# Block products for a second pair of chunks from tile 4 on, with new orders of work, in a fused FFN and long-convolution kernel

## The chip, the cores and the metric

The kernel runs on one core of a Trainium2 chip. The time is the device time of one execution in microseconds. The engines are PE (TensorE, matmuls), DVE (VectorE), ACT (ScalarE), POOL (GpSimd) and SP (SyncE, which here only issues DMAs). Each engine takes its instructions in the order of the program and waits on semaphores.

## The reference

x has 4 x 512 = 2048 tokens of 512 features. The result is x plus a long convolution plus a gated FFN, both of the layer-normed x:

```python
xn = _layernorm(x, axis=-1)
x = x + s4_convolution(xn) + ffn(xn)
# ffn, with NF4 weights of M = 1792, an absmax for each 64 codes:
g = jnp.einsum('bsh,mh->bsm', xn, Wg)
u = jnp.einsum('bsh,mh->bsm', xn, Wu)
h = jax.nn.silu(g) * u
out = jnp.einsum('bsm,hm->bsh', h, Wd)
# the convolution: its kernel K (512 long) is made from 64 complex poles,
# a Cauchy sum and an inverse FFT; y = irfft(rfft(u) * rfft(K)) + D * u
```

## The kernel before, in words

All products are made of three fp16 matmuls (high x high, high x low, low x high), so each weight and each activation is split into a high and a low half. M is cut into 14 tiles of 128 (k = 0 to 13), the tokens into four chunks of 512 (c = 0 to 3). For a tile and a chunk a gate product and an up product are wanted, of 12 matmuls of 128x512 each.

**Direct and block products.** For tiles 0 to 2 (the opening) all is direct. From tile 3 on, chunks 2 and 3 (side s = 0) are made together by seven block products of 6 matmuls in place of 8 (gate and up of two chunks taken as 2 x 2 blocks). Chunks 0 and 1 (side s = 1) have them from FIRST_BLOCKED[1] on, tile 5 in the kernel before. Block products need sums of the weights (up_sums, other_sums on DVE, then block_hi on ACT and block_lo on DVE) and, once, sums of the tokens of the pair: token_whole, token_sum and token_lo on DVE, token_hi on ACT, four of each for a side. Per tile and side ACT copies two products between banks (copy_m1, copy_m5) and DVE adds two (join). silu is on ACT, h_mul on DVE. The high half of h of chunk 0 is made by ACT (h_hi) where the chunk is direct, by POOL where it is blocked; h_lo is DVE's.

**Windows.** PE works through a mixed_window(k) while side 1 is direct, and a blocked_window(k) after that. In blocked_window(k) the order is products 1, then product 4 of the tile before, then 5, 6, 2, 3, 7, each for both sides; the first blocked window has no product 4. DVE, ACT and POOL each have an order written out by hand for the same windows.

**Units.** Each weight tile is a unit that is dequantised while earlier tiles multiply: SEQ lists the units, two for each of the tiles 3 to 12 (up of tile k+1, gate of tile k+2), then those of the down weights (GU and above). EARLY_IN names the windows in which one unit of the down weights is made in addition, so that made_in(k) is 3 there and 2 elsewhere; made_before(k) is the first unit of window k. For a unit SP loads codes (codes_of) and scales (absmax_of), POOL makes first_pass, ACT five or six passes (chain), DVE step WHOLE and step SCALED, POOL weight_hi (from unit 7 on, ACT before) and DVE weight_lo of the unit before. On POOL first_pass(u + 2) stands before weight_hi(u). On DVE the three operations of a unit are its items; eighths() spreads the items of a window over eight slots, and ACT's passes likewise.

**The load queue.** SP goes through the units in order:

```python
for place in range(8, UNITS - 3):
    codes_of(place + 1)
    if place > 8:
        absmax_of(place)
    if place == LINE_AT:
        toeplitz()
```

toeplitz() waits for the convolution's line (DVE, end of window 11), writes it to DRAM as 128 shifted copies (L629), waits until that has landed, and reads it back as the matrix T (L634). DVE takes T's maximum in the last slot of window 12 (L1894), then makes other_sums(13), block_lo(13, 0) and the joins of tile 12.

**The opening.** x is loaded in eight pieces of two token tiles (load_x). stats, moments and twelve small rstd steps for four token tiles give the normalisation; norm(t) applies it (ACT for t = 0, POOL for the others), turn(t) transposes a token tile on PE for t below 8, x_hi and x_lo split it. v_step and exp_step on POOL are small steps of 128x1 to 128x8 for the convolution's kernel.

## Time and profile before

| | us |
|---|---|
| median of 3 runs | 459.49 |
| lowest, highest | 458.85, 459.49 |
| profiled execution | 460.08 |
| its span | 458.3 |
| PE busy | 438.2 |
| DVE busy | 398.4 |
| ACT busy | 278.8 |
| POOL busy | 214.6 |

All times of rows are microseconds from the start of the span. A row of the timeline has the start, the duration, the engine (SPq is the load queue), the line of the kernel, the operation with its output and inputs, the count if several are merged, and in brackets the idle time before it with what ended that time. A helper has one line for all its calls, so an operation is told from its neighbours by its place in the order. A PE row's duration includes the drain of its last matmul.

### The profile page before, as it was taken

What the parts mean: (1) busy time and instruction counts of PE and PEld (TensorE: products, weight loads), DVE (VectorE), ACT (ScalarE), POOL (GpSimd) and SP (SyncE); (2) the same over time, 40 slices, a digit from 0 to 9 for tenths busy, and PEclk for the clock granted to TensorE, in tenths of its full rate; (3) what the DMA queues carried; (4) which work ended last, traced back from release to release, by engine and by line L of the source; (5) the groups of instructions that cost most, each with busy time, mean ns of one, the idle gap of its engine ahead of it and who ended that gap; (6) DMA issues with size and microseconds to landing.
All of it is one profiled execution on the core that took longest, in us unless ns stands there. A gap on an engine that the chain in (4) does not pass through costs nothing.

```text
span 458.3 us, 7272 instructions
## 1 busy us (share of the span) xinstructions
PE 438.2 (96%) x2560; PEld 248.8 (54%) x2560; DVE 398.4 (87%) x641; ACT 278.8 (61%) x472; POOL 214.6 (47%) x163
## 2 busy tenths in 40 slices
PE   1879999999999999999999999999999999999997
PEld 1534444443444444434444444466544788888886
DVE  5988979969889798999897879879996999999993
ACT  7868594295877759588684787856032542445340
POOL 2777299547456848669646847778100000000000
PEclk9989999999999999999999999999999999999999
DMA  8543636022315415155222233457691021101111
GB/s 291 172 131 139 144 75 182 1 92 71 138 47 183 161 47 200 54 183 191 63 69 65 61 80 101 111 187 249 193 369 60 1 94 47 46 1 48 47 47 46
DMA packets 34168, 51.41 MB, mean 112 GB/s; under 512 B 13076, under 2 KB 14164, under 8 KB 33364
## 3 DMA queue, kind: packets, MB, share of 16 engines
q1 hardware_dynamic: 34132, 50.95, 35.3%
q8 instruction: 20, 0.33, 0.3%
q14 instruction: 16, 0.13, 0.1%
HBM read 38.03 MB, written 10.81 MB: 107 GB/s over the span
## 4 chain that ended last, share of the span: by engine, by line
PE 85%; DVE 6%; ACT 2%; issue 2%; DMA 2%; POOL 1%; SPq 0%; DVEq 0%; ACTq 0%; POOLq 0%
PE bank L2264 33%; PE bank L2391 21%; PE bank L2109 16%; PE bank L2341 8%; PE bank L2331 6%; ACT work L936 1%; DMA h<-in_x 1%; DVE h L1438 1%; DVE work L1313 1%; DMA work<-in_q_gate 1%; DVE w L1323 1%; DVE work L1309 1%; PE bank L2145 0%; DVE h L1412 0%; POOL h L845 0%
## 5 line engine op out<-in xcount | busy, mean ns | idle before, releaser
L936 ACT ACTIVATE work<-work 128x512 f32<-128x512 f32 (+1 forms) x234 | 130.0, 628 | 11.5 <-POOL work L845 7.8
L845 POOL TENSOR_SCALAR work<-work 128x512 f32<-128x512 int32 x39 | 85.9, 2202 | 64.4 <-DVE work L1309 46.1
L2264 PE MATMUL bank<-h 128*128 128x512 f16 x360 | 81.5, 379 | 0.9 <-ACT bank L1029 0.9
L2109 PE MATMUL bank<-xT,w 128*128 128x512 f16 (+1 forms) x300 | 66.2, 377 | 2.3 <-DVE w L1323 1.1
L2264 PEld LDWEIGHTS bank<-h 128*128 128x128 f16 x360 | 34.9, 98 | 44.0 <-ACT bank L1029 2.4
L2391 PE MATMUL bank<-wd,work 128*128 128x256 f16 x504 | 56.2, 273 | 0.0
L2264 PE MATMUL bank<-xT,w 128*128 128x512 f16 x240 | 55.4, 379 | 0.0
L2391 PEld LDWEIGHTS bank<-wd,work 128*128 128x128 f16 (+1 forms) x504 | 49.3, 98 | 6.0
L2109 PEld LDWEIGHTS bank<-xT,w 128*128 128x128 f16 x300 | 29.4, 99 | 36.8 <-DVE w L1323 2.4
L1250 ACT ACTIVATE work<-h 128x896 f16<-128x896 f32 x30 | 27.9, 942 | 28.4 <-DVE h L2017 18.3
L2391 PE MATMUL bank<-h,work 128*128 128x256 f16 x378 | 42.2, 273 | 0.0
L858 POOL TENSOR_SCALAR w<-work,sc 128x512 f16<-128x512 f32 x21 | 39.0, 1857 | 6.6 <-DVE work L1313 5.6
L2391 PEld LDWEIGHTS bank<-h,work 128*128 128x128 f16 x378 | 37.0, 98 | 4.3
L2264 PEld LDWEIGHTS bank<-xT,w 128*128 128x128 f16 x240 | 23.4, 98 | 28.1
L2341 PE MATMUL bank<-wd,h 128*128 128x512 f16 x168 | 36.4, 379 | 0.0
L1309 DVE SCALAR_TENSOR_TENSOR work<-work 128x512 f32<-128x512 f32 x39 | 28.4, 729 | 5.1 <-ACT work L936 5.1
L2003 DVE TENSOR_TENSOR work<-h,work 128x896 bf16<-128x896 f32 x30 | 32.5, 1083 | 0.1
L1313 DVE SCALAR_TENSOR_TENSOR work<-work 128x512 f32<-128x512 f32 x41 | 29.9, 730 | 1.5
L1029 ACT ACTIVATE bank<-bank 128x512 f32<-128x512 f32 x20 | 11.6, 582 | 31.7 <-DVE work L1438 15.6
L1020 ACT ACTIVATE work<-bank,sc 128x512 f32<-128x512 f32 x36 | 24.6, 684 | 9.9 <-PE bank L2109 9.9
L2264 PE MATMUL bank<-xT,h 128*128 128x512 f16 x120 | 28.1, 379 | 1.2 <-DVE bank L1412 1.0
L858 POOL TENSOR_SCALAR wd<-work,sc 128x512 f16<-128x512 f32 x14 | 26.3, 1877 | 4.7 <-DVE work L1313 3.8
...
## 6 DMA issues: line engine op xcount, KB each, us to landing
...
```

The lines of the kernel that those rows point to most:

```text
L845: pool.tensor_scalar(chain_room(u, "r"), qs[:, u % 2, :], RIGHT_FROM, RIGHT_FROM, ALU.max, ALU.subtract).then_inc(first_done, 1)
L858: pool.tensor_scalar(weight_of(u)[HI], whole_of(u), scale_of(u), None, ALU.mult).then_inc(phi_done, 1)
L936: nc.scalar.activation(room, qs[:, u % 2, :] if j == 0 else room, KNEE, scale=scale, bias=bias, alpha=below).then_inc(knee_done, 1)
L1250: nc.scalar.activation(slot_of(o)[:, HI], src, ACT.Copy).then_inc(o_hi, 1)
L1309: ins = v.scalar_tensor_tensor(whole, left, CHAIN_TOP if u in CHAINED else LEFT_TOP, right, ALU.min, ALU.add)
L1313: ins = v.scalar_tensor_tensor(whole, whole, CHAIN_STEP if u in CHAINED else -LEFT_TOP, am[:, u % 2, :], ALU.add, ALU.mult)
L2003: v.tensor_tensor(slot[:, LO].bitcast(BF16), src, slot[:, HI], ALU.subtract).then_inc(o_lo, 1)
L2109: mm = nc.tensor.matmul(out_b, weights(k)[:, unit, wl, f, :], xT[:, TPC * c + first:TPC * c + last, xl, f, :], start=(i == 0), stop=(i == ...
L2264: mm = nc.tensor.matmul(out_b, weight(wl, f), token(xl, f), start=(n == 0 and i in (1, 5)), stop=(n == 5), skip_group_check=i not in (1, 5))
L2331: mm = nc.tensor.matmul(bank[(t + 4) % 8][:, P * j:HD], xT[:, t, xl, j, :], tz[:, tl, 0:HD - P * j], start=(n == 0), stop=(n == 3 * NC - 1))
L2341: mm = nc.tensor.matmul(bank[(t + 4) % 8][:], part, wd[:, mt, wl, :], start=(mt == 0 and n == 0), stop=(mt == NM - 1 and n == 2))
L2391: mm = nc.tensor.matmul(out_b, part, w, start=(n == 0), stop=(n == 3 * KT - 1))
```

## The change

FIRST_BLOCKED[1] becomes 4: side 1 has block products from tile 4 on. There is one mixed window now, that of tile 3. EARLY_IN becomes (7, 9, 11, 12): the window of tile 8 makes two units and that of tile 12 three. With it made_before(12), and so LINE_AT, become one less (30 and 31). The first token sum of side 1 stands in the opening, the other three and token_lo(1, 0) in tile 3. In tile 3 weight_lo(9) stands before the steps of unit 10 (LO_SOONER). In the windows of two blocked sides h_mul of chunk 0 stands behind one slot of items instead of two. In the opening ACT makes norms 0, 1 and 4 (ACT_NORMS), POOL the others; x 2 and 3 are loaded later; the gate product of tile 1 stands before turn(4) on PE; stats, scales, weight halves and passes stand in another order; warm_up has 12 matmuls instead of 16; and the first fourteen v_steps on POOL stand behind first_pass(8).

```diff
@@ -39,7 +39,7 @@
 BLOCKED = range(3, NM)
 BLOCKS = (1, 5, 2, 6, 3, 7, 4)
 ROLE_B, ROLE_E = (2, 0), (3, 1)
-FIRST_BLOCKED = (3, 5)
+FIRST_BLOCKED = (3, 4)
 A_BANK, E_BANK, B_BANK = (4, 0), (5, 1), (6, 2)
@@ -119,7 +119,7 @@
-EARLY_IN = (7, 8, 9, 11)
+EARLY_IN = (7, 9, 11, 12)
 EARLY = len(EARLY_IN)
 SEQ = list(range(9))
 for k in range(3, NM - 1):
@@ -560,7 +560,12 @@
         RSTD = 12
         SUMMED = (1,)
-        POOL_NORMS = 1
+        ACT_NORMS = (0, 1, 4)
+        LO_SOONER = made_before(3) + 1
+
+        def pool_norms(t):
+
+            return t + 1 - sum(1 for i in ACT_NORMS if i <= t)
         ACC = 4
         WEIGHT_SCALES = 9
@@ -662,11 +667,11 @@
             load_x(1)
             load_codes(1, q_up[0])
             sp.dma_start(amf, am_flat).then_inc(amf_ld, 16)
-            load_x(2)
-            load_x(3)
             load_absmax(0, am_gate[0])
             load_codes(2, q_gate[1])
+            load_x(2)
             load_absmax(1, am_up[0])
+            load_x(3)
             load_codes(3, q_up[1])
             load_absmax(2, am_gate[1])
             sp.dma_start(cols[:], s4_cols).then_inc(s4_ld, 16)
@@ -867,16 +872,15 @@
                 pool.tensor_scalar(sums_room(SEQ[u] // 2)[0], whole_of(u), scale_of(u), None, ALU.mult).then_inc(g_done, 1)
             first_pass(1)
-            for t in range(POOL_NORMS, TPC):
-                norm(t)
+            norm(2)
+            norm(3)
             first_pass(2)
             first_pass(3)
             first_pass(4)
-            for t in range(TPC, 2 * TPC):
-                norm(t)
+            norm(5)
+            norm(6)
+            norm(7)
             first_pass(5)
-            for i in range(14):
-                v_step(i)
             first_pass(6)
             for t in range(2 * TPC, 3 * TPC):
                 norm(t)
@@ -884,6 +888,8 @@
             for t in range(3 * TPC, NT):
                 norm(t)
             first_pass(8)
+            for i in range(14):
+                v_step(i)
             for i in range(EXP_STEPS):
                 exp_step(i)
             for u in POOL_HALVES:
@@ -1037,7 +1043,7 @@
                 act.wait_ge(xs_done[s], (1, 3, 2, 4)[i])
                 if i == 0:
                     if s == 0:
-                        act.wait_ge(xp_done, NT - POOL_NORMS)
+                        act.wait_ge(xp_done, pool_norms(NT - 1))
                     else:
                         act.wait_ge(xlo_done, NT)
                 nc.scalar.activation(tk[s][:, i, HI].rearrange("p f t -> p (f t)"), x_sums[s][(1, 2, 0, 3)[i]],
@@ -1067,7 +1073,7 @@
                                      ACT.Copy).then_inc(hhi_done, 1)
             def norm(t):
-                act.wait_ge(rs_step, RSTD)
+                act.wait_ge(rs_step, RSTD * (t // TPC + 1))
                 nc.scalar.activation(xnb[:, t % 8, :], xs[:, t, :], ACT.Identity, scale=rs[:, 4, t:t + 1],
                                      bias=rs[:, 5, t:t + 1]).then_inc(xn_done, 1)
@@ -1090,7 +1096,7 @@
                     act.wait_ge(tp_done, t + 1)
                     src, dst = bank[4 + t % TPC][:], xT[:, t, HI].rearrange("p c f -> p (c f)")
                 else:
-                    act.wait_ge(xp_done, t - POOL_NORMS + 1)
+                    act.wait_ge(xp_done, pool_norms(t))
                     src, dst = xnb[:, t % 8, :], xst[:, t % 8, HI, :]
                 nc.scalar.activation(dst, src, ACT.Copy).then_inc(xhi_done, 1)
@@ -1099,11 +1105,12 @@
             stats(1)
             chain(1, 0, 5)
             norm(0)
+            norm(1)
             chain(1, 5, 6)
+            chain(2, 0, 1)
+            weight_hi(0)
             x_hi(0)
-            weight_hi(0)
             x_hi(1)
-            chain(2, 0, 1)
             x_hi(2)
             x_hi(3)
             chain(2, 1, 2)
@@ -1111,25 +1118,26 @@
             chain(2, 2, 6)
             chain(3, 0, 2)
             weight_hi(2)
-            chain(3, 2, 4)
+            chain(3, 2, 6)
+            norm(4)
+            silu(0)
+            act.wait_ge(b_mm, 1)
+            nc.scalar.activation(yv[:, 0:2], bank[3][:, 0:2], ACT.Copy).then_inc(b_cp, 1)
+            weight_hi(3)
             x_hi(4)
-            chain(3, 4, 6)
-            silu(0)
-            chain(4, 0, 1)
-            weight_hi(3)
+            chain(4, 0, 2)
             x_hi(5)
             x_hi(6)
-            act.wait_ge(b_mm, 1)
-            nc.scalar.activation(yv[:, 0:2], bank[3][:, 0:2], ACT.Copy).then_inc(b_cp, 1)
             x_hi(7)
-            chain(4, 1, 6)
+            chain(4, 2, 6)
+            silu(1)
             h_hi(0)
-            silu(1)
+            chain(5, 0, 3)
             weight_hi(4)
-            chain(5, 0, 6)
+            chain(5, 3, 6)
             h_hi(1)
+            x_hi(8)
             silu(2)
-            x_hi(8)
             weight_hi(5)
             x_hi(9)
             x_hi(10)
@@ -1169,26 +1177,18 @@
             def mixed_window(k):
                 n = NCH * k
-                if k > 3:
-                    silu(n)
-                    copy_m1(0, k)
-                    part(k, 0, 2)
                 h_hi(n)
                 copy_m5(0, k)
-                if k == 3:
-                    items(ACT_AT[9] - 3, ACT_AT[9])
-                    part(k, 0, 2)
-                else:
-                    token_hi(1, 0)
-                part(k, 2, 3)
+                items(ACT_AT[9] - 3, ACT_AT[9])
+                part(k, 0, 3)
                 silu(n + 2)
                 part(k, 3, 5)
                 silu(n + 1)
+                token_hi(1, 0)
                 part(k, 5, 6)
                 silu(n + 3)
                 part(k, 6, 8)
-                if k > 3:
-                    part(k + 1, 0, 2)
+                part(k + 1, 0, 2)
                 block_hi(k + 1, 0)
                 block_hi(k + 1, 1)
@@ -1327,7 +1327,7 @@
                 for p in range(first, last):
                     u, i = item_of(DVE_AT, p)
                     if u in CHAINED:
-                        i = (3, 4, 2)[i]
+                        i = ((2, 3, 4) if u == LO_SOONER else (3, 4, 2))[i]
                     if i != 2:
                         step(u, i if i < 2 else i - 1)
                     elif u > 0:
@@ -1377,7 +1377,7 @@
                 if s == 0 and f == 0:
                     dve.wait_ge(xt_ld[c - 2], 16 * TPC)
                 elif s == 1 and i == 2:
-                    dve.wait_ge(xp_done, NT - POOL_NORMS)
+                    dve.wait_ge(xp_done, pool_norms(NT - 1))
                 elif s == 1 and i == 0:
                     dve.wait_ge(xt_ld[1], 16 * TPC)
                 hi, lo = (xT[:, TPC * c:TPC * c + TPC, l, f:f + 2, :] for l in (HI, LO))
@@ -1566,64 +1566,64 @@
             rstd(0, 3)
             rstd(0, 4)
             rstd(0, 5)
-            step(0, WHOLE)
+            scales(1)
             rstd(0, 6)
             rstd(0, 7)
             rstd(0, 8)
-            scales(1)
+            scales(2)
             rstd(0, 9)
-            scales(2)
+            scales(3)
             rstd(0, 10)
-            scales(3)
+            scales(4)
             rstd(0, 11)
-            scales(4)
             dve.wait_ge(id_done, 1)
             scales(5)
-            stats(4)
             scales(6)
+            step(0, WHOLE)
             step(0, SCALED)
-            step(1, WHOLE)
             scales(7)
             scales(8)
+            step(1, WHOLE)
+            weight_lo(0)
             x_lo(0)
-            weight_lo(0)
             x_lo(1)
             step(1, SCALED)
             x_lo(2)
             x_lo(3)
             weight_lo(1)
+            stats(4)
             stats(5)
             stats(6)
+            step(2, WHOLE)
+            step(2, SCALED)
             stats(7)
             moments(4, 8)
+            weight_lo(2)
             rstd(1, 0)
             rstd(1, 1)
             rstd(1, 2)
             scales(9)
             rstd(1, 3)
+            scales(10)
             rstd(1, 4)
+            scales(11)
             rstd(1, 5)
-            step(2, WHOLE)
+            scales(12)
             rstd(1, 6)
             rstd(1, 7)
             rstd(1, 8)
-            step(2, SCALED)
+            step(3, WHOLE)
             rstd(1, 9)
             rstd(1, 10)
             rstd(1, 11)
-            weight_lo(2)
+            step(3, SCALED)
+            h_mul(0)
+            weight_lo(3)
             stats(8)
             x_lo(4)
-            scales(10)
-            step(3, WHOLE)
-            scales(11)
-            step(3, SCALED)
-            h_mul(0)
-            scales(12)
-            weight_lo(3)
+            stats(9)
             x_lo(5)
             x_lo(6)
-            stats(9)
             x_lo(7)
             stats(10)
             stats(11)
@@ -1648,13 +1648,13 @@
             step(5, WHOLE)
             step(5, SCALED)
             h_lo(1)
+            x_lo(8)
             stats(12)
-            x_lo(8)
-            stats(13)
             weight_lo(5)
             x_lo(9)
             x_lo(10)
             x_lo(11)
+            stats(13)
             h_mul(2)
             stats(14)
             stats(15)
@@ -1703,6 +1703,7 @@
             token_lo(0, 2)
             token_whole(1, 1)
             h_mul(10)
+            token_sum(1, 0)
             token_lo(0, 1)
             weight_lo(7)
             up_sums(BLOCKED[0], 7)
@@ -1718,34 +1719,24 @@
                     items(eighths(DVE_AT, k, first), eighths(DVE_AT, k, last))
                 n = NCH * k
-                if k == 3:
-                    h_mul(n)
-                    h_lo(n)
-                    join(0, k, 0)
-                    part(0, 5)
-                    join(0, k, 1)
-                    h_mul(n + 3)
-                    part(5, 6)
-                else:
-                    part(0, 2)
-                    token_sum(1, 1)
-                    h_mul(n)
-                    part(2, 3)
-                    h_lo(n)
-                    part(3, 4)
-                    join(0, k, 0)
-                    token_sum(1, 2)
-                    token_lo(1, 0)
-                    part(4, 6)
-                    join(0, k, 1)
-                    h_mul(n + 3)
-                token_sum(1, 0 if k == 3 else 3)
+                h_mul(n)
+                h_lo(n)
+                join(0, k, 0)
+                part(0, 2)
+                token_sum(1, 1)
+                part(2, 5)
+                join(0, k, 1)
+                h_mul(n + 3)
+                token_sum(1, 2)
+                token_lo(1, 0)
+                part(5, 6)
                 part(6, 7)
                 other_sums(k + 1)
                 h_mul(n + 1)
                 block_lo(k + 1, 0)
                 h_mul(n + 2)
                 block_lo(k + 1, 1)
+                token_sum(1, 3)
                 part(7, 8)
             def window(k, stage=None):
@@ -1763,9 +1754,9 @@
                     h_mul(n + 1)
                     block_lo(k, 1)
                     h_mul(n + 2)
-                    stage_of(0, 2)
+                    stage_of(0, 1)
                     h_mul(n)
-                    stage_of(2, 4)
+                    stage_of(1, 4)
                     join(0, k, 0)
                     stage_of(4, 5)
                     h_lo(n)
@@ -2135,25 +2126,25 @@
             nc.tensor.transpose(bank[0][0:3, 0:P], amx, ident[:]).then_inc(mx_tp, 1)
             def turn(t):
-                if t < POOL_NORMS:
-                    pe.wait_ge(xn_done, t + 1)
-                else:
-                    pe.wait_ge(xp_done, t - POOL_NORMS + 1)
+                if t in ACT_NORMS:
+                    pe.wait_ge(xn_done, ACT_NORMS.index(t) + 1)
+                else:
+                    pe.wait_ge(xp_done, pool_norms(t))
                 if t >= TPC:
                     pe.wait_ge(xlo_done, t - TPC + 1)
                 for f in range(NC):
                     mm = nc.tensor.transpose(bank[4 + t % TPC][:, P * f:P * f + P], xnb[:, t, P * f:P * f + P], ident[:])
                 mm.then_inc(tp_done, 1)
-            warm_up(10)
-            turn(0)
+            warm_up(8)
             pe.wait_ge(one_done, 1)
             pe.wait_ge(sc_done, 7)
             nc.tensor.matmul(bank[0][:, P:P + 6], ones[:], dg3, start=True, stop=True).then_inc(mx_bc, 1)
+            turn(0)
             turn(1)
             turn(2)
             turn(3)
-            warm_up(6)
+            warm_up(4)
             pe.wait_ge(wlo_done, 1)
             pe.wait_ge(xlo_done, 2)
@@ -2165,8 +2156,8 @@
             for i in range(2):
                 mm = nc.tensor.matmul(bank[3][:, i:i + 1], vcs[:, P * i:P * i + P], bps, start=True, stop=True)
             mm.then_inc(b_mm, 1)
+            products(1, (0,))
             turn(4)
-            products(1, (0,))
             turn(5)
             turn(6)
             turn(7)
```

## Rows read from the trace of the kernel before

**Rows 1.** The page: busy time, share of the span and instructions of each engine.

```profile
PE 438.2 (96%) x2560; PEld 248.8 (54%) x2560; DVE 398.4 (87%) x641; ACT 278.8 (61%) x472; POOL 214.6 (47%) x163
```

**Rows 2.** PE's waits, whole span: line, releaser: us, times, longest.

```profile
PE bank L2145 <- POOL h L749: 2.9, 1, 2.9
PE bank L2109 <- DVE w L1323: 1.1, 1, 1.1
PE bank L2264 <- DVE bank L1412: 1.0, 1, 1.0
PE bank L2264 <- ACT bank L1029: 0.9, 1, 0.9
```

**Rows 3.** Busy time by stretch: PE, PEld, DVE, ACT, POOL, clock, DMA, GB/s.

```profile
83.00:90.00 7.00, 7.00 (x34) 3.14 (x32) 7.00 (x9) 0.84 (x2) 3.61 (x2) 1.00 0.00 0
...
143.04:161.17 18.13, 18.13 (x85) 8.23 (x84) 15.21 (x26) 13.03 (x25) 14.16 (x9) 1.00 0.45 151
...
179.66:200.11 20.45, 18.47 (x85) 8.05 (x84) 18.99 (x30) 15.82 (x31) 15.63 (x9) 1.00 0.38 124
```

**Rows 4.** One microsecond of the opening: PE busy, granted clock, DMA.

```profile
28.00:29.00 1.00, 1.00 (x3) 0.50 0.00 0
```

**Rows 5.** Timeline of the opening: start, us, engine, line, operation, count, idle.

```profile
25.74 1.09 DVE L1323 SCALAR_TENSOR_TENSOR w<-work,sc,w 128x512 f16<-128x512 f32 x1 [0.32 <-ACT w L963]
26.88 4.45 PE L2109 MATMUL bank<-xT,w 128*128 128x512 f16 x12
...
33.01 12.26 PE L2109 MATMUL bank<-xT,w 128*128 128x512 f16 x56 [0.37 <-ACT yv L1123]
...
34.24 0.68 DVE L1551 TENSOR_TENSOR xT<-bank,xT 128x512 f16<-128x512 f32 x1
```

**Rows 6.** Timeline: small steps and weight halves on POOL, weight_lo(7) on DVE.

```profile
34.62 0.29 POOL L805 TENSOR_SCALAR V<-yv,cols 128x2 f32<-128x2 f32 x1
...
72.20 2.39 POOL L771 TENSOR_SCALAR sc<-sc 128x1 f32<-128x1 f32 x1
...
76.30 0.19 POOL L775 TENSOR_TENSOR sc<-sc 128x1 f32<-128x1 f32 x1
...
79.48 2.24 POOL L858 TENSOR_SCALAR w<-work,sc 128x512 f16<-128x512 f32 x1
...
88.61 0.74 DVE L1323 SCALAR_TENSOR_TENSOR w<-work,sc,w 128x512 f16<-128x512 f32 x1
```

**Rows 7.** Timeline: a token sum, block_lo(3,0), and PE's products 5 and 6 of tile 3.

```profile
80.86 1.21 DVE L1395 TENSOR_TENSOR h<-h 128x1024 f32<-128x1024 f32 x1
...
92.66 0.58 DVE L1369 SCALAR_TENSOR_TENSOR h<-h,sc 128x256 f16<-128x256 f32 x1
...
93.89 2.75 PE L2264 MATMUL bank<-h 128*128 128x512 f16 x12
```

**Rows 8.** Timeline: h_mul of chunk 0 in tile 8's window.

```profile
188.36 0.74 DVE L1438 SCALAR_TENSOR_TENSOR work<-bank,sc,h 128x512 f32<-128x512 f32 x1
```

**Rows 9.** Timeline of the load queue: issues around the line's transfer (L629).

```profile
254.70 1.10 SPq L609 DMA_DIRECT2D work<-in_am_down  x2
257.25 0.32 SPq L629 DMA_DIRECT2D lines<-wd  x1
...
271.13 0.37 SPq L603 DMA_DIRECT2D work<-in_q_down  x1
```

**Rows 10.** Timeline of tile 12's end and tile 13's beginning.

```profile
273.31 0.69 DVE L1894 TENSOR_REDUCE sc<-wd 128x1 f32<-128x512 f32 x1 [2.20 <-DMA wd<-lines]
...
274.23 1.95 POOL L845 TENSOR_SCALAR work<-work 128x512 f32<-128x512 int32 x1 [5.34 <-DMA work<-in_q_down]
...
275.46 0.68 DVE L1412 TENSOR_TENSOR h<-bank,h 128x512 f32<-128x512 f32 x1
...
276.27 2.08 POOL L858 TENSOR_SCALAR wd<-work,sc 128x512 f16<-128x512 f32 x1
...
278.25 2.75 PE L2264 MATMUL bank<-h,w 128*128 128x512 f16 x12
```

## The prediction

> **What bounds the kernel now.** I read the busy times first: TensorE (PE) is busy 96% of the span [rows 1]. Then PE's waits, longest first [rows 2]: 2.9 us in the opening for a normalised tile from POOL, 1.1 us for a low weight half from DVE (tile 4), and 1.0 and 0.9 us for DVE's join and ACT's copy (both in tile 8). Past 33 us PE waits for about 3.5 us in all, so the kernel is a chain of matmuls with four small holes. The stretches by stage say who is nearly late [rows 3]: DVE is busy 7.00 of 7 us before tile 3 and 18.99 of 20.45 in tile 8, while tile 6 (18.13 us for 14 products of 6 matmuls, so 0.216 us a matmul) has 3 us of DVE to spare. So every edit is read twice: what it does to PE, and whether DVE, POOL or the load queue (SP) can still serve PE. The profiled execution took 460.08 us (span 458.3), 0.59 above the median of 459.49; I sum differences from it and put them on the median.
>
> **Fewer matmuls.** Chunks 0 and 1 of tile 4 took 48 matmuls directly and take 7 x 6 = 42 as block products: 6 x 0.216 = -1.3 us on PE, which is the bound. ACT gets four copies where it had two and loses one h_hi to POOL; DVE gets two joins. These lie in the spare time of tile 5's kind of window, which had no PE wait.
>
> **The opening.** Before, PE stood 2.9 us for turn(4), then ran the twelve gate matmuls at a mean of 0.37 us instead of 0.216 [rows 5], with the granted clock at 0.50, which is 1.2 of 2.4 GHz [rows 4]: 1.8 us more. Now the gate product stands ahead of turn(4). I followed the three queues with this trace's durations (0.6 to 0.7 us for an operation of 128x512 on ACT or DVE, 0.86 for a norm on POOL, 0.1 to 0.2 for the four-column steps). On DVE weight_lo(1) ends near 19.1; stats 4 to 6 take 1.9, step 2's two operations 1.4, stats(7) and moments 1.0, and weight_lo(2) ends near 24.0 (before at 26.8 [rows 5]). PE's gate product runs from 24.1 to 26.7. rstd, now behind weight_lo(2), ends near 26.6; turn(4) waits a microsecond for ACT's norm; three norms on POOL end at 29.5 and turn(7) at 30.0. ACT makes x_hi(4), two passes and x_hi 5 to 7 by 32.4, and x_lo(7), which ended at 34.92 [rows 5], ends near 33.4. Chunk 1 can then start at 33.5 instead of 35.6 (33.01 [rows 5] and twelve matmuls): -2.1 us. DVE itself leads by only about 1.6. What I don't see is whether the clock falls again; if it does, the wait for x_lo(7) hides half of it. Bounds: 0.8 to 2.6 us. The cutting of norms to ACT, the later loads of x 2 and 3 (they are read only near 19 us) and the new place of stats cost nothing beyond this.
>
> **The DVE debt before tiles 3 and 4.** token_sum(1,0), 1.2 us like its like [rows 7], now stands before token_lo(0,1), in a stretch where DVE has no idle time [rows 3]. Product 5 of tile 3 started at 93.89, and block_lo(3,0), its last input, ended at 93.24 [rows 7]: 0.65 us of slack. PE comes 2.1 earlier, DVE 1.6 earlier and 1.2 later: a wait of 1.1. In tile 3 DVE gets three more operations of 1.2 us, of which its idle time before the second join hides one or two; block_lo(4,0) then comes 1.0 us late for product 5 of tile 4, and token_lo(1,1) 0.9 late for product 6. The wait of 1.1 us for weight_lo(9) goes, since unit 9 is wanted a window later. Sum to the end of tile 4: -2.1 - 1.3 - 1.1 + 1.1 + 1.0 + 0.9 = -1.5 us.
>
> **Fourteen small POOL steps.** v_step 0 to 13 leave the time at 33 us, where one took 0.29 us, for the place between first_pass(8) and the seventeen exp steps. There a step of the same size took 2.39 us, beside two of DVE's 1.2 us operations [rows 6]. Giving each POOL step the DVE operation that it meets, the exp steps end at 86 to 87 instead of 76.5 [rows 6], first_pass(9) and weight_hi(7) follow, and weight_hi(7), which ended at 81.7 [rows 6], ends near 91.2 on the old axis. DVE wants it for weight_lo(7), which stood at 88.61 [rows 6], now at 89.8. So the old slack of 6.9 us is gone, and 1.4 us more; a little of it is idle time of DVE later in tile 3: DVE, and PE with it, +1.2. Bounds: 0 (each step at 0.29 us, 4.1 us, hidden) to +2.5. The Trainium skill ("GPSIMD Engine Reference", Specifications) says that POOL's way into SBUF is shared with VectorE and is contended by VectorE instructions with two SBUF inputs. The trace agrees (2.39 against 0.29); a reader who held the steps to be free would leave the 1.2 us out.
>
> **Tiles 7 to 9.** Tile 8's window makes two units instead of three, and h_mul of chunk 0, which stood at 188.36 [rows 8] behind two items, now follows h_mul(n+2) at once, some 3 us sooner. ACT's copy comes sooner with it: the 0.9 us goes. Of the 1.0 us for the join, DVE gets 1.4 us back, but PE asks 0.9 sooner: 0.3 to 0.6 may stay. Together -1.6 (bounds -1.3 and -2.0). Tile 9 keeps three units.
>
> **Tile 12, which the change's words don't name.** EARLY_IN now has 12, so window 12 makes units 30, 31 and 32 (before: 31 and 32), and LINE_AT, made_before(12) + 1, falls from 32 to 31. SP thus stops for toeplitz() one unit earlier. Before, the scales of unit 32 went out at 254.70, then the line at 257.25; SP waited for it and only then sent codes, at 271.13, 13.9 us later [rows 9]. Now the codes of unit 33 and the scales of unit 32 are those that wait, while window 12 still needs both: step(32, SCALED) the scales, and weight_hi(31), which stands behind first_pass(33) on POOL, the codes. On the old axis: codes land at 274.2, first_pass runs 274.23 to 276.2, weight_hi 276.27 to 278.35, as unit 34's and 32's did [rows 10]; weight_lo(31) ends at 279.1. Only then comes the maximum of T, which stood at 273.31: DVE is 5.8 us late. The first join behind it stood at 275.46 and took 0.68; it ends at 281.9. Product 4 of tile 12, which waits for that join, stood at 278.25: PE waits 3.7 us. Behind it DVE is ahead again for what product 6 wants. Bounds: 3.0 and 4.5 (ACT's silu and block_hi stand behind the passes of unit 33). Nothing covers this: PE has no other work ahead in its queue.
>
> **The clock there.** PE would stand still in two pieces, with kernel_max between. After 2.9 us of standing in the opening the clock went to 0.50 and cost 1.8 us; here it is 0 to 1.8. I take 0.8. The Trainium skill ("TensorE: Matmul & The Clock Gate", Part 1) has the gate fall to half after an idle stretch, by which the full 1.8 would be due: the sum would be 3.6 and not 2.6.
>
> **Sum.** -1.5 + 1.2 - 1.6 + 3.7 + 0.8 = +2.6 us: 462.7 for a profiled execution like this one, 462.1 for the median.
>
> **Rivals.**
> (a) *Late loads decide, as above*: 461 to 463.5, chance 0.46.
> (b) *Late loads, but POOL's steps are hidden and the clock stays up*: -1.5 - 1.6 + 3.7 = +0.6, 460.1; chance 0.22, half of it within 0.2%. For it: at the pace of 33 us all fourteen take 4.1 us, inside the slack of 6.9. Against: the 2.39.
> (c) *Faster*: the wait at tile 12 doesn't reach PE, because the line's transfer is done sooner or ends before DVE asks. -1.5 - 1.6 with 0 to 1.2 for POOL: 456.4 to 457.6; chance 0.20. For it: DVE idled 2.2 us before T anyway. Against: the order of the queues leaves no way around the 13.9 us.
> (d) *Slower still*: POOL late by 2.5, the full 1.8 of the clock: -1.5 + 2.5 - 1.3 + 3.7 + 1.8 = +5.2, 464.7; chance 0.12. It decides where weight_hi(7) ends later than 92.
>
> The range must leave out no more than 2 in 10: from 457.0 (inside c) to 464.5 (inside d). A difference of 0.2%, 0.9 us, is about what a measurement of this kernel can tell from none. Faster: c and a little of b, 0.21. Same: 0.12. Slower: 0.67.
>
> **What would show it.** A wait of PE of 3 us or more near tile 12's product 4, with SP's codes behind the line's transfer; exp steps that end past 84; no wait of PE in tile 8 over 0.6; chunk 1 starting near 33.5; waits near 1 us at product 5 of tiles 3 and 4. If PE runs through window 13 without a hole, the prediction is wrong at its largest term and the time is near 457. If the opening gives more than 3 us, DVE was not the bound that I make it.

## The result, and the profile after

The changed kernel took 472.63 us (median; 471.01 to 474.97) against 459.17 for the kernel before beside it: a ratio of 1.030, 95% interval 1.025 to 1.034. The forecast was 462.1 with a range of 457.0 to 464.5. The direction was right; the size was missed by 10.5 us, and the time lies outside the range. The profiled execution has a span of 470.6 us, 12.3 more than before.

The page after, busy times, answers [rows 1]. TensorE (PE) has 10 matmuls less in the records (six by the block products, four by the shorter warm_up) and yet 3 us more busy time, in the main by the half clock: 24 matmuls of tile 4 and twelve of tile 12 took 1.7 and 1.5 us more than at full clock. Its share fell from 96 to 94%.

```profile
PE 441.2 (94%) x2550; PEld 249.3 (53%) x2550; DVE 400.4 (85%) x643; ACT 282.6 (60%) x475; POOL 222.5 (47%) x162
```

PE's waits after answer [rows 2] (line, releaser: us in total, times, longest). The 2.9 us for POOL's norm in the opening are gone; 14.2 us of others stand in these rows: for the block's low half (L1369), for joins (L1412, five small ones and a long one), for weight halves (L1323, one of them 1.17 us in the opening) and for the maximum of T (L1885).

```profile
PE bank L2255 <- DVE h L1369: 5.2, 2, 3.8
PE bank L2255 <- DVE bank L1412: 3.3, 5, 1.4
PE bank L2100 <- DVE w L1323: 2.6, 2, 1.4
PE bank L2255 <- DVE h L1412: 2.2, 1, 2.2
...
PE bank L2199 <- DVE sc L1885: 0.9, 1, 0.9
```

Two stretches after, as in [rows 3] (PE, PEld, DVE, ACT, POOL, granted clock, DMA share, GB/s). PE is full in both and runs 6 or 7 matmuls where 9 fit: the clock is at 1.2 of 2.4 GHz.

```profile
116.00:118.00 2.00, 2.00 (x7) 0.65 (x5) 2.00 (x3) 1.94 (x4) 0.00 (x0) 0.50 0.03 8
290.00:292.00 2.00, 2.00 (x6) 0.61 (x5) 1.90 (x4) 1.48 (x3) 0.00 (x0) 0.50 0.41 131
```

**Where the time came from.** I set PE's milestones of the two traces side by side. Chunk 1 starts 1.1 us sooner (34.47 for 35.6). Product 5 of tile 3 is 2.0 late (95.92 against 93.89 [rows 7]); the start of tile 6, 5.5 (148.59 against 143.04 [rows 3]); that of tile 9, 5.2; that of tile 12, 7.0 (264.32 for 257.28); the ones of tile 13, 7.25; and behind product 4 of tile 12 it is 12.1. So there are three places: tiles 3 and 4, tiles 10 and 11, and the line's transfer.

Tiles 3 and 4, timeline after (start, us, engine, line, operation, shape, count, idle before and its releaser):

```profile
73.89 11.46 POOL L776 TENSOR_SCALAR sc<-sc 128x1 f32<-128x1 f32 x9
...
88.89 1.58 POOL L863 TENSOR_SCALAR w<-work,sc 128x512 f16<-128x512 f32 x1
90.51 1.20 DVE L1323 SCALAR_TENSOR_TENSOR w<-work,sc,w 128x512 f16<-128x512 f32 x1 [4.07 <-POOL w L863]
...
91.76 2.76 PE L2100 MATMUL bank<-xT,w 128*128 128x512 f16 x12 [1.43 <-DVE w L1323]
...
110.86 0.68 DVE L1309 SCALAR_TENSOR_TENSOR work<-work 128x512 f32<-128x512 f32 x1
...
111.71 2.02 POOL L850 TENSOR_SCALAR work<-work 128x512 f32<-128x512 int32 x1 [5.46 <-DVE work L1309]
...
113.76 0.63 ACT L942 ACTIVATE work<-work 128x512 f32<-128x512 f32 x1 [1.49 <-POOL work L850]
114.30 0.49 ACT L1063 ACTIVATE h<-h,sc 128x256 f16<-128x256 f32 x1
...
114.82 0.48 DVE L1369 SCALAR_TENSOR_TENSOR h<-h,sc 128x256 f16<-128x256 f32 x1 [1.48 <-ACT h L1063]
...
115.45 7.03 PE L2255 MATMUL bank<-h 128*128 128x512 f16 x24 [3.83 <-DVE h L1369]
```

The fourteen moved steps take 6.4 us (60.7 to 67.1) where they took 3.2 in their old place. The nine at 73.9 aren't among them: they are exp steps, which stood behind first_pass(8) in the kernel before too and took 9.19 us there (from 66.75). Pushed back by the fourteen, they take 11.5 us, while VectorE runs operations of 1024 columns with two inputs. POOL's high half of unit 7 ends at 90.47 in place of 81.7 [rows 6], and VectorE stands 4.07 us for it. At 110.86 a chain starts that names five instructions on three engines: unit 10's W (step WHOLE) on VectorE, POOL's first pass of unit 12, unit 12's pass on ScalarE, and only behind it the block's high half (L1063) and low half (L1369). PE waits 3.83 us for the last and then has 24 matmuls in 7.03 us, where they take 5.34.

The line's transfer after, answering [rows 9] and [rows 10] (SP issues the loads):

```profile
264.50 0.32 SPq L634 DMA_DIRECT2D lines<-wd  x1
...
277.89 0.36 SPq L639 DMA_DIRECT2D wd<-lines  x1
278.35 0.38 SPq L608 DMA_DIRECT2D work<-in_q_down  x1
278.78 1.11 SPq L614 DMA_DIRECT2D work<-in_am_down  x2
...
281.41 1.93 POOL L850 TENSOR_SCALAR work<-work 128x512 f32<-128x512 int32 x1 [4.75 <-DMA work<-in_q_down]
...
283.43 1.57 POOL L863 TENSOR_SCALAR wd<-work,sc 128x512 f16<-128x512 f32 x1
283.72 0.94 DVE L1313 SCALAR_TENSOR_TENSOR work<-work 128x512 f32<-128x512 f32 x1 [4.75 <-DMA work<-in_am_down]
...
285.71 0.68 DVE L1885 TENSOR_REDUCE sc<-wd 128x1 f32<-128x512 f32 x1
...
288.89 4.21 PE L2255 MATMUL bank<-h,w 128*128 128x512 f16 x12 [2.18 <-DVE h L1412]
```

Codes and scales of window 12's units go out 13.9 us behind the line. POOL and VectorE both stand 4.75 us for them, the maximum of T follows them, and PE waits 0.89 and 2.18 us and then runs twelve matmuls in 4.21 us instead of 2.75 [rows 10].

### The profile page after: what moved, and what is told of

Its sections match the earlier page's. It is cut to its first block, busy times and chain, and to the rows that moved or that the text cites. A ratio compares the mean times of both kernels' runs of the same rounds, so it can differ in the third digit from the quotient of the medians.

```text
span 470.6 us, 7259 instructions
## 1 busy us (share of the span) xinstructions
PE 441.2 (94%) x2550; PEld 249.3 (53%) x2550; DVE 400.4 (85%) x643; ACT 282.6 (60%) x475; POOL 222.5 (47%) x162
## 3 DMA queue, kind: packets, MB, share of 16 engines
q1 hardware_dynamic: 34132, 50.95, 34.6%
## 4 chain that ended last, share of the span: by engine, by line
PE 60%; POOL 13%; issue 11%; DVE 10%; ACT 3%; DMA 2%; SPq 0%; DVEq 0%; POOLq 0%; ACTq 0%
PE bank L2255 26%; PE bank L2382 20%; PE bank L2332 8%; PE bank L2322 6%; POOL work L850 4%; POOL sc L776 2%; POOL h L754 2%; ACT work L942 2%; DVE w L1323 1%; DMA h<-in_x 1%; POOL w L863 1%; DVE work L1309 1%; DVE bank L1412 1%; DVE wd L1789 1%; DVE work L1313 1%
## 5 line engine op out<-in xcount | busy, mean ns | idle before, releaser
L850 POOL TENSOR_SCALAR work<-work 128x512 f32<-128x512 int32 x39 | 84.3, 2161 | 74.5 <-DVE work L1309 58.9
L2255 PE MATMUL bank<-h 128*128 128x512 f16 x378 | 87.1, 385 | 5.2 <-DVE h L1369 5.2
L2255 PEld LDWEIGHTS bank<-h 128*128 128x128 f16 x378 | 37.4, 99 | 52.1 <-issue 7.6
L2255 PE MATMUL bank<-xT,w 128*128 128x512 f16 x252 | 58.0, 379 | 0.0
L2100 PE MATMUL bank<-xT,w 128*128 128x512 f16 (+1 forms) x252 | 53.7, 369 | 3.7 <-DVE w L1323 2.6
L863 POOL TENSOR_SCALAR w<-work,sc 128x512 f16<-128x512 f32 x21 | 41.9, 1996 | 6.2 <-DVE work L1313 5.2
L2100 PEld LDWEIGHTS bank<-xT,w 128*128 128x128 f16 x252 | 24.2, 98 | 31.6 <-DVE w L1323 3.2
L2255 PEld LDWEIGHTS bank<-xT,w 128*128 128x128 f16 x252 | 24.6, 98 | 29.5
L2255 PE MATMUL bank<-h,w 128*128 128x512 f16 x126 | 30.7, 392 | 2.3 <-DVE h L1412 2.2
L2255 PE MATMUL bank<-xT,h 128*128 128x512 f16 x126 | 29.7, 379 | 3.3 <-DVE bank L1412 3.3
L1026 ACT ACTIVATE work<-bank,sc 128x512 f32<-128x512 f32 x35 | 23.8, 679 | 11.9 <-PE bank L2100 10.8
```

What stands on the lines that cost most here:

```text
L850: pool.tensor_scalar(chain_room(u, "r"), qs[:, u % 2, :], RIGHT_FROM, RIGHT_FROM, ALU.max, ALU.subtract).then_inc(first_done, 1)
L863: pool.tensor_scalar(weight_of(u)[HI], whole_of(u), scale_of(u), None, ALU.mult).then_inc(phi_done, 1)
L2100: mm = nc.tensor.matmul(out_b, weights(k)[:, unit, wl, f, :], xT[:, TPC * c + first:TPC * c + last, xl, f, :], start=(i == 0), stop=(i == ...
L2255: mm = nc.tensor.matmul(out_b, weight(wl, f), token(xl, f), start=(n == 0 and i in (1, 5)), stop=(n == 5), skip_group_check=i not in (1, 5))
```

## The experiments

Each edit is on the changed kernel unless it says otherwise. "Median" is of the execution times; 472.6 is the changed kernel, 459.2 to 460.2 the kernel before beside them. By the 95% intervals of the ratios most of these medians are good to 1 or 2 us and a few to almost 3, so a difference of 3 us between two runs is uncertain by 2 to 3. The stretches of the traces, set side by side behind the runs, are sharper. Where the expectations of runs 11 and 12 call the ScalarE steps ahead of the block's high half unit 10's, they are unit 12's.

**1. The place of the line's transfer.**

```diff
-LINE_AT = made_before(NM - 2) + 1
+LINE_AT = made_before(NM - 2) + 2
```

> The changed kernel with one edit: the load queue meets the line's transfer one unit later (after unit 32, as before the change). Theory A (the queue order makes the hole at tile 13's beginning): PE's two waits there (0.9 and 2.2 us) and the stretch at half clock behind them (1.6 us) go, and with the lengthened first matmuls some 5.0 us: 467.6 against 472.6. Rival (DVE is simply too full in window 12 with three units, whoever loads when): the waits only move, and less than 1 us goes.

476.49 us (476.2 to 477.58): 4 us slower, a miss. The timeline of this run:

```profile
272.91 1.10 SPq L614 DMA_DIRECT2D work<-in_am_down  x2
...
274.06 0.53 SPq L634 DMA_DIRECT2D lines<-wd  x1
...
286.83 0.36 SPq L639 DMA_DIRECT2D wd<-lines  x1
...
289.53 0.69 DVE L1885 TENSOR_REDUCE sc<-wd 128x1 f32<-128x512 f32 x1 [7.81 <-DMA wd<-lines]
...
290.27 0.27 PE L2199 MATMUL bank<-ident,sc 128*1 128x128 f32 x1 [4.55 <-DVE sc L1885]
...
292.50 5.10 PE L2255 MATMUL bank<-h,w 128*128 128x512 f16 x12 [1.96 <-DVE h L1412]
```

With a third unit in window 12, the scales of unit 32 find their room free only at 272.9, 8.4 us behind the 264.50 at which the line went in the changed kernel; whichever goes first, the other is late. T's read follows the line by 12.8 us, about as before (13.4). So moving the line cures nothing while the third unit is there; run 2 takes that away.

**2. The third unit back to tile 8.**

```diff
-EARLY_IN = (7, 9, 11, 12)
+EARLY_IN = (7, 8, 9, 11)
```

> The edit: EARLY_IN back to (7, 8, 9, 11), all else as in the changed kernel. Theory A (with the third unit in tile 12, the line's transfer, the read of T, the codes and the scales stand behind one another in the DMA queue and cost 3.4 us at product 4 of tile 12 and about 1.6 us of half clock behind it): TensorE's gain from the start of tile 13's ones to its fives is as before the change (about 5.3 us less 0.2), the time 472.6 - 5.0 = 467.6 us, plus up to 1 us that tile 8 asks for with its third unit: 467.6 to 468.6. Theory B (the tail is late since everything ahead of it is late, whichever tile has the third unit): the wait at product 4 stays over 1.5 us and the time is 471 us or more.

468.24 us (467.57 to 470.46): -4.4, theory A. The wait for the maximum of T is gone. T's maximum and product 4 in this run; product 4 has no wait and the full clock:

```profile
282.71 0.69 DVE L1885 TENSOR_REDUCE sc<-wd 128x1 f32<-128x512 f32 x1 [2.40 <-DMA wd<-lines]
...
286.89 2.75 PE L2255 MATMUL bank<-h,w 128*128 128x512 f16 x12
```

**3. The fourteen small steps** back behind `first_pass(5)`, where they stood.

```diff
 first_pass(5)
+for i in range(14):
+    v_step(i)
 first_pass(6)
...
 first_pass(8)
-for i in range(14):
-    v_step(i)
```

> The changed kernel with one edit: the fourteen small POOL steps back behind first_pass(5). Theory A (POOL's late weight_hi(7) holds up DVE by 4.1 us, and DVE then PE): DVE's wait for it is gone, PE's waits in tile 3 (1.4 and 1.4 us) fall to one of at most 1 us, and the 3.8 us wait in tile 4 shrinks by what DVE has gained: 3 to 6 us less, 466.6 to 469.6. Rival (tile 4's wait is ACT's own queue order and swallows what DVE gains): only 1.8 us or less goes, and tile 4's wait grows.

469.52 us (466.42 to 471.84): -3.1. Unit 7's halves in this run:

```profile
76.69 2.24 POOL L863 TENSOR_SCALAR w<-work,sc 128x512 f16<-128x512 f32 x1
...
86.97 0.74 DVE L1323 SCALAR_TENSOR_TENSOR w<-work,sc,w 128x512 f16<-128x512 f32 x1
```

POOL is 8 us ahead of VectorE again and tile 3 has no wait: from the start of chunk 1 to product 5 of tile 3 PE takes 58.29 us, as in the kernel before, against 61.45. Tile 4's wait stays at 3.5 us; theory A had it shrink.

**4. The same steps alone, in the kernel before**, moved from behind `first_pass(5)` to behind `first_pass(8)`.

```diff
 first_pass(5)
-for i in range(14):
-    v_step(i)
...
 first_pass(8)
+for i in range(14):
+    v_step(i)
```

> The edit: the kernel before, and in it alone the fourteen small steps of the tables moved from behind unit 5's first pass to behind unit 8's on POOL. Theory A (they are 14 in a row with 0.2 to 0.3 us each and stand right ahead of unit 7's high half there, which VectorE waits for): unit 7's low half comes 3 to 4 us later, TensorE waits 1.5 to 3 us in tile 3, 461.5 to 462.5 us. Theory B (POOL has the time there, as the +1.2 of the sum took it, and only the pair's earlier token sums make the wait): 459.2 to 460.5 us.

463.91 us (462.74 to 465.15) against 460.08: +3.8, theory A, 1.4 us above its upper end. Its timeline:

```profile
76.72 11.46 POOL L771 TENSOR_SCALAR sc<-sc 128x1 f32<-128x1 f32 x9
...
92.47 1.20 DVE L1323 SCALAR_TENSOR_TENSOR w<-work,sc,w 128x512 f16<-128x512 f32 x1 [4.34 <-POOL w L858]
```

Here the pair is as before, so the steps alone make this wait. By the medians of the two runs the term is 3.1 and 3.8 us; by PE's stretch from chunk 1 to product 5 of tile 3 it is 3.2 in the changed kernel, 3.4 in this run, and up to 4.6 in the other runs that have the steps in the new place.

**5. h_mul of chunk 0** in its old place, behind two items of VectorE instead of one.

```diff
-stage_of(0, 1)
+stage_of(0, 2)
 h_mul(n)
-stage_of(1, 4)
+stage_of(2, 4)
```

> The changed kernel with one edit: h_mul of chunk 0 again behind two slots of items instead of one in the windows of two blocked sides. Theory A (moved up, it waits for product 4 in windows 10 and 11 and holds DVE and POOL's small copies up): the waits of 0.6 and 1.0 us at the joins of tiles 10 and 11 go, that of tile 8 (1.4) stays or grows by 0.9: 0.5 to 2 us less. Rival (those waits come from the units' other places, not from h_mul): no change, or up to 1 us more because ACT's copy is late again in tile 8.

469.54 us (469.11 to 469.87): -3.1, more than expected. PE's waits for the bank's join (L1412) in this run, beside the 3.3 us in five of the changed kernel:

```profile
PE bank L2255 <- DVE bank L1412: 1.0, 1, 1.0
```

The joins that went, 2.3 us in all, lie in the windows of tiles 7 to 11; that of tile 8 fell from 1.41 to 0.99. Product 4 of tile 5 to that of tile 11 takes PE 113.06 us in this run, 115.92 in the changed kernel and 114.24 before, so h_mul's move alone costs 2.9 us there, and without it the lighter window of tile 8 would have gained 1.2. In the changed kernel POOL's eight copies of the turned rows start 6.6 us later than before (251.53 for 244.94), where PE is 5.9 later, and take 2.68 us instead of 2.02; h_lo waits behind them:

```profile
251.53 2.68 POOL L843 COPY wd<-wd 128x4 f32<-128x4 f32 x8 [7.05 <-DVE wd L1789]
...
256.93 0.69 DVE L1450 TENSOR_TENSOR h<-work,h 128x512 bf16<-128x512 f32 x1 [3.01 <-POOL h L832]
...
260.43 1.47 PE L2255 MATMUL bank<-xT,h 128*128 128x512 f16 x6 [0.96 <-DVE bank L1412]
```

With the old place the copies take 2.02 us and h_lo waits 1.48 again.

**6. The pair from tile 5 on again**, with all the new orders kept (with them come the old mixed windows).

```diff
-FIRST_BLOCKED = (3, 4)
+FIRST_BLOCKED = (3, 5)
```

> The edit: FIRST_BLOCKED back to (3, 5), with the mixed windows of the kernel before for tiles 3 and 4 (the first token sum of side 1 stays in the opening); the opening's new order, EARLY_IN (7, 9, 11, 12), h_mul's new place and the fourteen small steps behind unit 8's first pass stay. Theory A (the pair from tile 4 on saves 1.3 us of matmuls and 1.1 us of a wait, and costs 3.8 us of waiting for the block's low half and 1.7 us of half clock): 472.6 - 3.1 = 469.5 us, with the wait for unit 7's low half in tile 3 still there (1 to 2 us) and the tail as in the changed kernel. Theory B (the pair itself is worth what it saves, and the orders alone are at fault): 472.6 + 1.3 to 2.4 = 474 to 475 us.

470.38 us (469.51 to 470.95): -2.2, nearer to A (-3.1) than to B (+1.3 or more). So the pair from tile 4 on, in the order that the change gives it, costs more than its six matmuls and the spared wait bring. The trace has more of it: from product 5 of tile 3 to product 4 of tile 5 PE takes 50.51 us in place of 55.26; 1.3 of these 4.7 us it had lost ahead of that stretch, where it waited longer for unit 7.

**7. The token sums at an eighth of their width.**

```diff
+if s == 1 and i > 0:
+    made, one, two = made[:, 0:128], one[:, 0:128], two[:, 0:128]
 v.tensor_tensor(made, one, two, ALU.subtract)
```

> The edit: on the changed kernel, the second to fourth token sums of side 1 are made for 128 of their 1024 columns, so that each takes about 0.2 us of VectorE in place of 1.21; the sums left out make side 1's block products wrong. Theory A (VectorE's work in tile 3 is what makes the block's low half of tile 4 late): each of the two sums that stand ahead of it there takes 1 us off VectorE, and the wait of 3.8 us falls by 1 to 2 us, with as much off the time: 470.6 to 471.6 us. Theory B (the wait hangs on ScalarE and POOL alone, behind the silu of chunk 3 and POOL's first pass): the wait stays at 3.4 us or more and the time at 472 to 473 us.

470.46 us (470.18 to 472.62), -2.2; the wait for the block's low half falls from 3.8 to 2.9 us. Theory A a little under its lower end in the wait (0.9 where it had 1 to 2) and in the time: two of the sums are ahead of it on VectorE, but VectorE had stood idle 1.39 us between them, so only the second counts whole.

**8. ScalarE's high halves of tile 4 sooner.**

```diff
 part(k, 6, 8)
-part(k + 1, 0, 2)
 block_hi(k + 1, 0)
 block_hi(k + 1, 1)
+part(k + 1, 0, 2)
```

> The changed kernel with one edit: in tile 3's window ACT makes block_hi(4, 0) and (4, 1) ahead of the first passes of unit 12, not behind them. Theory A (block_hi stands behind a pass that waits for POOL's first_pass(12), which waits for DVE's step WHOLE of unit 10): the 3.8 us wait at product 5 of tile 4 falls under 1.2 and the half clock behind it (1.7 us) goes: 4 to 5 us less, 467.6 to 468.6. Rival (DVE is the bound there: its four token operations make block_lo late anyway): under 1 us goes.

471.79 us (470.83 to 472.45): -0.8. Theory A missed; the rival's size is the one that came. The high half now starts at 109.37 instead of 114.30, 4.9 us sooner, and the low half at 113.45 instead of 114.82: VectorE has the token's low half, unit 9's low half, W of unit 10 and the other sums ahead of it. PE waits 2.27 us in place of 3.83, and the half clock stays. Two queues held the low half back; with ScalarE's out of the way, VectorE's own order still lets it start only 1.4 us sooner.

**9. Both queues, the block's halves ahead of everything**, the token's low half last. The ScalarE part is that of 8; VectorE's:

```diff
-token_lo(1, 0)
-part(5, 6)
-part(6, 7)
 other_sums(k + 1)
-h_mul(n + 1)
 block_lo(k + 1, 0)
-h_mul(n + 2)
+part(5, 6)
+h_mul(n + 1)
 block_lo(k + 1, 1)
+h_mul(n + 2)
+part(6, 7)
+token_lo(1, 0)
```

> The edit: at tile 3, ScalarE makes the two high halves of tile 4's block sums ahead of the first steps of the next unit, and VectorE makes the other sums and both low halves ahead of the token sum's low half and of unit 10's W (part 6 to 7 behind them). Theory A (in VectorE's and ScalarE's order, W, POOL's first pass and ScalarE's chain stand ahead of the block's low half, and TensorE waits 3.8 us for it and then runs 12 matmuls at half clock, 1.7 us): both go, 472.6 - 5.2 = 467.4 us, and TensorE's wait at the first block product of tile 4 is under 0.8 us. Theory B (the time is only lent: unit 10's W comes 2 us later, POOL's next first pass with it, and the wait comes back in tile 5): 471 to 473 us, with a new wait of 2 us or more between the starts of tiles 5 and 6.

477.15 us (474.47 to 480.26): +4.5, theory B and worse than it. The timeline:

```profile
112.23 1.46 PE L2255 MATMUL bank<-h 128*128 128x512 f16 x6
...
114.53 1.22 DVE L1400 TENSOR_TENSOR h<-h 128x1024 f16<-128x1024 f32 x1
...
114.78 4.50 POOL L850 TENSOR_SCALAR work<-work 128x512 f32<-128x512 int32 x1 [7.76 <-DVE work L1309]
...
115.90 2.52 PE L2255 MATMUL bank<-h 128*128 128x512 f16 x6 [2.21 <-DVE h L1400]
...
120.48 5.52 PE L2255 MATMUL bank<-h 128*128 128x512 f16 x12 [2.06 <-ACT bank L1035]
```

The wait for the block's low half is gone. In its place PE waits for the token's low half (L1400), which I had put last, and for ScalarE's copy (L1035), which stands behind a step that waits for POOL's first pass; and that pass takes 4.50 us beside two of VectorE's 1024-column operations.

**10. Four cures at once**: 2, 3, 5 and 9 together.

> The edit: four at once on the changed kernel: the fourteen small steps back behind unit 5's first pass, h_mul of chunk 0 back to its old place, EARLY_IN back to (7, 8, 9, 11), and the block's halves of tile 4 sooner on ScalarE and VectorE. The pair of chunks from tile 4 on and the opening's order stay. Theory A (the four causes are apart, and each wait goes with its own): 472.6 - 3.1 - 3.0 - 5.0 - 4.0 = 457.5 us, from 456 to 460, faster than the kernel before by 0 to 0.7%. Theory B (the waits are one shortage of VectorE and POOL that comes back elsewhere): 464 us or more.

465.53 us (463.48 to 467.06). By the time this is theory B (464 us or more). But against run 9 the three undone edits give 477.15 - 465.53 = 11.6 us, where singly they give 10.6; so these three are apart, and what fails here is run 9's order: PE still waits 2.1 us for the token's low half and 3.1 for ScalarE's copy.

**11. A better order for tile 4, with the other three undone**: on VectorE the token's low half, then the other sums and both low halves, then units 9 and 10; on ScalarE `part(4, 0, 2)` stands in tile 4's window, behind `copy_m1` and `token_hi(1, 1)`. VectorE's part:

```diff
 token_lo(1, 0)
-part(5, 6)
-part(6, 7)
 other_sums(k + 1)
-h_mul(n + 1)
 block_lo(k + 1, 0)
-h_mul(n + 2)
+h_mul(n + 1)
 block_lo(k + 1, 1)
+part(5, 6)
+part(6, 7)
+h_mul(n + 2)
```

> The edit: the pair from tile 4 on and the new opening stay; the fourteen small steps are back behind unit 5's first pass, h_mul of chunk 0 in its old place, EARLY_IN (7, 8, 9, 11). At tile 3 VectorE makes the token sum's low half, then the other sums and the block's two low halves, then unit 9's and 10's steps; ScalarE makes the block's high halves without a step of unit 10's chain ahead of them, and that chain's first steps stand behind the copies of the first block products of tile 4. Theory A (what was late in the run with these four cures was the token sum's low half, 2.1 us, and the copies behind POOL's first pass, 3.1 us; both are ahead of it now): 465.5 - 4 = 461.5 us, 460 to 463. Theory B (VectorE and POOL are short in tiles 3 and 4 in whatever order, and the wait moves to unit 9's low half or unit 10's weights): 465 us or more.

459.72 us (458.94 to 461.64, ten runs), ratio 0.9997 (0.9981 to 1.0014): theory A, 1.8 us better than its figure and 0.3 below its range. The block's low half is in time; two shorter waits are left:

```profile
108.09 2.75 PE L2255 MATMUL bank<-h 128*128 128x512 f16 x12
...
112.13 1.47 PE L2255 MATMUL bank<-h 128*128 128x512 f16 x6 [1.29 <-ACT bank L1035]
...
115.19 1.46 PE L2255 MATMUL bank<-h 128*128 128x512 f16 x6 [1.59 <-DVE h L1400]
```

**12. That order alone** (VectorE's and ScalarE's part of run 11, and nothing else).

> The edit: on the changed kernel, only tile 3's order on VectorE and ScalarE for the block sums of tile 4 (the other sums and the low halves ahead of unit 9's and 10's steps; unit 10's first ScalarE steps behind the copies). The fourteen small steps, h_mul and EARLY_IN stay as in the changed kernel. Theory A (the wait of 3.8 us and the 1.7 us of half clock behind it come from the order of these two queues, and 2.9 us of shorter waits take their place): 472.6 - 5.5 + 2.9 = 470 us, 469.3 to 471, and the granted clock in tile 4 is 1.00. Theory B (tile 4's wait is fed by unit 7's lateness at tile 3, so that it goes only with the fourteen steps): the wait at the first block product of tile 4 is over 2.5 us and the time 471.5 us or more.

469.65 us (466.90 to 470.71): -3.0, theory A. Tile 3 still has its 2.13 us for unit 7, and product 5 of tile 4 starts 3.8 us later than in run 11; the two waits of tile 4 are the same 1.29 and 1.59:

```profile
111.91 2.75 PE L2255 MATMUL bank<-h 128*128 128x512 f16 x12
115.95 1.47 PE L2255 MATMUL bank<-h 128*128 128x512 f16 x6 [1.29 <-ACT bank L1035]
119.01 1.46 PE L2255 MATMUL bank<-h 128*128 128x512 f16 x6 [1.59 <-DVE h L1400]
```

So tile 4's wait doesn't come from tile 3's lateness; it is made by the order of its own queues.

**13. The last two waits**, on run 11.

```diff
 block_lo(k + 1, 1)
+h_mul(n + 2)
+token_sum(1, 3)
 part(5, 6)
 part(6, 7)
-h_mul(n + 2)
-token_sum(1, 3)
```

> The edit: on the run with the pair from tile 4 and its halves ahead of unit 9's and 10's steps, h_mul of chunk 2 of tile 3 and the fourth token sum of side 1 stand ahead of these steps too. Theory A (what is left at tile 4 are 1.29 us for the copies of the first block products, which ScalarE makes only behind that h_mul, and 1.59 us for the low half of a token sum, which is 2.3 us behind its sum): both shrink, to 0.5 us in all, and the time is 459.7 - 2.4 = 457.3 us, level with the run that has the pair from tile 5 and less matmuls still to save; Theory B (unit 10's W comes 1.9 us later, POOL's first pass with it, and a later token half or unit 10's weights make a wait of the same size): 459 to 461 us.

461.37 us (460.88 to 461.80): 1.7 slower than run 11, theory B. The copies are in time, and the next token's low half makes a wait of 2.69 us and a join one of 1.3, where there had been 2.9 in all. In neither of the two orders does VectorE serve the pair there in time; a third wasn't tried.

**14. The opening alone**: the changed kernel with the pair from tile 5 on, and 2, 3 and 5 undone.

> The edit: the changed kernel with the pair from tile 5 on again (FIRST_BLOCKED (3, 5) and the mixed windows of before), EARLY_IN (7, 8, 9, 11), h_mul of chunk 0 in its old place and the fourteen small steps back behind unit 5's first pass. What stays is the opening's new order on the queues, on ScalarE, VectorE and TensorE, with the first token sum of side 1 in the opening. Theory A (the opening brings the 1.1 us by which chunk 1 started sooner, and nothing behind it takes them back): 459.5 - 1.1 = 458.4 us, 457.5 to 459. Theory B (what the runs so far took away adds up: 472.6 - 3.1 - 3.1 - 4.4 - 2.2 = 459.8, so the opening is worth nothing at the end): 459.5 to 460.5 us.

457.11 us (456.57 to 457.83), ratio 0.9936 (0.9916 to 0.9956): faster than both kernels, and 1.3 us better than A (0.4 below its range). PE's waits in this run; beside them stands only the opening's:

```profile
PE bank L2274 <- DVE bank L1420: 1.0, 1, 1.0
PE bank L2274 <- ACT bank L1035: 0.9, 1, 0.9
```

Product 5 of tile 3 comes 1.6 us sooner than before (92.31 against 93.89), and tile 4's, 2.8 sooner (111.74 for 114.55): the wait of 1.1 us for unit 9's low half [rows 2] is gone too. LO_SOONER stayed, which I had not counted in A: that low half stands at 103.11 here and stood at 110.80.

## Why the prediction was wrong

The undone parts add up. Runs 2, 3, 5 and 12 take away 4.4, 3.1, 3.1 and 3.0 us, 13.6 in all; 472.6 - 13.6 is 459.0, and run 11, which undoes all four, took 459.7. The traces say the same without the spread of the medians. The table cuts the span of one execution of each kernel at PE's milestones (us from one to the next), with the terms of the forecast that fall there:

| PE's stretch | forecast | before | changed | run 11 | run 14 |
|---|---|---|---|---|---|
| to the start of chunk 1 | -2.1 | 35.60 | 34.47 | 34.17 | 34.03 |
| to product 5 of tile 3 | +2.3 | 58.29 | 61.45 | 58.30 | 58.28 |
| to product 4 of tile 5 | -0.5 | 51.74 | 55.26 | 52.66 | 50.51 |
| to product 4 of tile 11 | -1.6 | 114.24 | 115.92 | 114.24 | 114.23 |
| to product 4 of tile 12 | +3.7 | 18.38 | 21.79 | 18.38 | 18.38 |
| to the end | +0.8 | 180.0 | 181.7 | 180.0 | 180.0 |

**Opening, -2.1, and the wait in tile 4, -1.1: right in sum for run 14, in part by luck.** Together they were -3.2, and run 14, which holds them and little else, is at -3.0. But there the wait went because unit 9's low half stands earlier, and not, as the term had it, because unit 9 is wanted a window later. The opening itself was overrated by half: chunk 1 starts 1.1 us sooner in the changed kernel. By the trace the gate product starts at 24.82 where I had it at 24.1, x_lo(7) ends at 34.4 instead of 33.4; among the runs with this opening the gate product starts at 23.8 to 24.9 and chunk 1 at 33.6 to 34.6, so the miss is hardly more than that. The clock didn't fall there: its twelve matmuls took 2.76 us instead of 4.45 [rows 5].

**Fourteen small steps, +1.2 with a bound of 2.5: wrong in size.** It was 3.1 to 3.8. The mechanism was as told (the exp steps ended at 86.8 where I had 86 to 87, weight_hi(7) at 90.5 where I had 91.2), but I let VectorE's idle time in tile 3 take most of it back. VectorE had none to give ahead of the block's low half: unit 7's low half started 1.9 us late and lengthened from 0.74 to 1.20 us beside POOL, and the block's low half behind it came 2.65 late (95.31 for 92.66 [rows 7]). The lateness was paid at two waits, 1.43 and 1.39. The +1.1 for product 5 of tile 3, for the token sum moved into the opening, was nothing by itself: in the five runs that have that sum there and the steps back, the stretch takes 58.3 us, as before. So the two terms together were +2.3 for a measured +3.2. Rival (b), that the steps are hidden, fell.

**Block product 5 of tile 4, +1.0, and product 6, +0.9: the step that failed most.** From product 5 of tile 3 to the start of tile 6 the sum had -0.5, and the trace has +3.5. I counted how late VectorE would be and left ScalarE's queue out. The diff also puts `part(k + 1, 0, 2)` ahead of block_hi at tile 3, and the sum has no term for it. That is a wait for POOL's first pass, this for unit 10's W, and W stands behind the token's sum and low half on VectorE: a loop over three queues, 3.83 us, and 1.7 of half clock behind it. The wait of 0.9 for product 6 didn't come. Run 12 takes 3.0 us off by the order alone (2.6 by the stretch); runs 8 and 9 show that neither one queue nor a hasty order of both does it. The -1.3 for the six matmuls is real work saved, but in the orders tried the pair is a loss even so: run 11 has it and takes 2.6 us more than run 14, which has not (2.2 by the stretch).

**Tiles 7 to 9, -1.6: wrong in sign.** The copy's 0.9 went, as told, but PE gained only 0.3 to the start of tile 9 and lost 0.7 and 1.1 in tiles 10 and 11, for which the sum had nothing: a miss of 3.1. The join of tile 8, which was to wait 0.3 to 0.6 us and no more, waited 1.41. The part of the term that was right is the lighter window of tile 8: in run 5, with h_mul back and that window kept, PE gains 1.2 us. h_mul's move turned it into a loss. I had priced the move by what becomes ready sooner and not by what is queued behind it on VectorE: W of the next unit waits with it; POOL's pass, its copies and h_lo follow.

**Tile 12, +3.7, and the clock, +0.8: right in path and size, the clock's part too small.** The waits came as 0.89 and 2.18 us with 1.5 of half clock behind them; milestone to milestone, product 4 is 3.4 later and what follows it 4.8. Run 2 gives back 4.4. Of the clock nearly the full price was due and not 0.8, as the sentence behind that term had it: the Trainium skill ("TensorE: Matmul & The Clock Gate", Part 1) has the gate fall after an idle stretch. This trace agrees (0.50 from 290 to 292, behind the wait of 2.18 us); other waits as long left the clock up (see the last section). What I then got wrong was the cure (run 1).

**The range.** Rival (d) was a little more of the same terms. No rival had a second queue in tile 4, nor a loss from h_mul, and the bounds of the range were those of each term's one mechanism. Two terms, tile 4 and tiles 7 to 9, failed the same way: an instruction moved on one engine was priced without the queues behind it, and together they were 7.1 of the 9.7 us between the sum of +2.6 and the +12.3 of the trace.
